# Gate logits of a macaron block from one 16-column product, added by stacked identities

## The reference

```python
x = x + 0.5 * ffn(layernorm(x), ...)
x = x + attn(layernorm(x), ...)
x = x + 0.5 * ffn(layernorm(x), ...)

def ffn(x, gamma1, Wq, bq, Wdown, bdown, Wup, bup, Wo, bo, gamma2, Wg, bg, We):
    h = rmsnorm(x, gamma1)
    q = (h @ Wq + bq).reshape(b, t, 16, 16)
    kv = ((h @ Wdown + bdown) @ Wup + bup).reshape(b, t, 16, 32)
    k, v = split(kv)
    att = softmax(einsum('bthd,btgd->bthg', q, k) / 4)
    out = einsum('bthg,btgd->bthd', att, v).reshape(b, t, 256)
    x = x + (out @ Wo + bo)
    h2 = rmsnorm(x, gamma2)
    gate = softmax(h2 @ Wg + bg)                      # 8 experts, all used
    return x + einsum('btd,edf,bte->btf', h2, We, gate)
```

## Time and profile before

| | |
|---|---|
| timed runs (3) | 1108.99 us median, 1102.47 to 1110.01 |
| the profiled execution | 1103.58 us, span 1101.7 us |
| mean granted TensorE clock | 0.99 of full |
| PE busy | 1031.2 us, 94% |
| DVE busy | 871.4 us, 79% |
| POOL busy | 725.8 us, 66% |
| ACT busy | 653.9 us, 59% |
| DMA moved | 14.30 MB, mean 13 GB/s |

### The profile page before, as it was taken

One profiled execution on the slowest core, in us unless ns is written; L12 is line 12 of the kernel. 1 busy time (PEld: TensorE's weight loads), 2 busy tenths in 40 slices (PEclk: granted clock), 3 DMA queues, 4 the chain that ended last, 5 costly groups with the idle time before them and its releaser, 6 DMA issues. The chain is left out here.

```text
span 1101.7 us, 28470 instructions
## 1 busy us (share of the span) xinstructions
PE 1031.2 (94%) x11320; PEld 779.0 (71%) x11320; DVE 871.4 (79%) x1372; ACT 653.9 (59%) x1331; POOL 725.8 (66%) x727
## 2 busy tenths in 40 slices
PE   4699999999999989999999999877999999999997
PEld 3577878888888855556556556456778788888785
DVE  7888778687785379999998999986886786876853
ACT  4565465565664457767777676654654655655642
POOL 8677476475554348788778887984574664755544
PEclk9899999999999999999999999998999999999999
DMA  6210000000000000000000000000000000000000
GB/s 196 69 40 1 1 2 1 2 1 2 2 2 1 1 1 2 2 1 2 1 1 2 1 2 1 2 1 2 2 2 21 21 2 20 21 1 21 21 1 39
DMA packets 8411, 14.30 MB, mean 13 GB/s; under 512 B 2516, under 2 KB 6102, under 8 KB 8280
## 3 DMA queue, kind: packets, MB, share of 16 engines
q1 hardware_dynamic: 8280, 12.47, 3.4%
HBM read 8.28 MB, written 4.19 MB: 11 GB/s over the span
## 5 line engine op out<-in xcount | busy, mean ns | idle before, releaser
L444 PE MATMUL psum<-we,h 128*128 128x512 f32 x1536 | 397.3, 402 | 0.3 <-DVE X L1062 0.3
L444 PEld LDWEIGHTS psum<-we,h 128*128 128x128 f32 x1536 | 275.6, 188 | 59.4 <-issue 2.3
L1417 POOL TENSOR_TENSOR late<-late 128x512 f32<-128x512 f32 x64 | 82.5, 1290 | 160.0 <-ACT late L1241 160.0
L1241 ACT ACTIVATE late<-psum,gate 128x256 f32<-128x256 f32 x256 | 107.2, 471 | 136.0 <-PE psum L444 96.0
L1089 DVE TENSOR_REDUCE oT<-psum 128x128 fp32r<-128x1024 f32 x128 | 155.5, 1217 | 30.0 <-PE psum L811 30.0
L1062 DVE SCALAR_TENSOR_TENSOR X<-psum,gate,X 128x256 f32<-128x256 f32 x256 | 122.8, 481 | 65.3 <-PE psum L444 55.7
L1291 ACT ACTIVATE kvx<-psum 128x1024 f32<-128x1024 f32 x128 | 131.2, 1025 | 70.5 <-PE psum L821 67.9
L1455 POOL TENSOR_TENSOR kvx<-kvx,late 128x2048 f32<-128x2048 f32 x32 | 124.4, 3887 | 34.3 <-ACT late L1298 34.3
L1095 DVE TENSOR_REDUCE late<-kvx 128x256 f32<-128x2048 f32 x64 | 145.7, 2276 | 0.0
L1455 POOL TENSOR_TENSOR late<-kvx,late 128x2048 f32<-128x2048 f32 x32 | 124.5, 3891 | 29.1 <-ACT late L1298 29.1
L821 PE MATMUL psum<-oT,neg_id 128*128 128x512 f32 x256 | 93.7, 447 | 18.1 <-DVE oT L1089 17.6
(11 more groups left out here) (152 smaller groups left out, 1980.8 us busy)
## 6 DMA issues: line engine op xcount, KB each, us to landing
X<-in_L_attn_hidden_states SPq DMA_DIRECT2D x8, 512.0 KB, 5.9
out<-X SPq DMA_DIRECT2D x8, 512.0 KB, 2.6
X<-in_L_ffn_We SPq DMA_DIRECT2D x2, 1024.0 KB, 10.8
kvx<-in_L_ffn_Wq SPq DMA_DIRECT2D x1, 256.0 KB, 3.2
kvx<-in_L_ffn_Wup SPq DMA_DIRECT2D x2, 128.0 KB, 3.0
kvx<-in_L_ffn_Wo SPq DMA_DIRECT2D x1, 256.0 KB, 4.4
X<-in_L_attn_Wk SPq DMA_DIRECT2D x1, 256.0 KB, 2.8
X<-in_L_attn_Wq SPq DMA_DIRECT2D x1, 256.0 KB, 3.6
```

The source lines that it names most:

```text
L444: ins = e.matmul(out_ap, l, r, start=(n == 0 and not opened), stop=(n == len(terms) - 1), skip_group_check=opened)
L1241: e.activation(y[:, n // 2 * 2 + w, :], psum[:, u % 3, w * D:(w + 1) * D], ACT.Copy, scale=gate[k % 2][:, i, 2 * n + w:2 * n + w + 1]).the ...
L1417: own.step(e.tensor_tensor(y[:, 0:2, :], y[:, 0:2, :], y[:, 2:4, :], ALU.add))
```

## The change

`wg` is laid out so that for each half kk the rounded weights and their rest lie side by side, 16 columns. The gate takes two products for each kk (rounded h2 and the rest of h2, each by all 16 columns) instead of three, into 16 partitions: partitions 0 to 7 hold the part with rounded weights and the bias, 8 to 15 the part with the rest of the weights. (One small term, rest by rest, is now in the sum; before it was left out.) `bgate` has 16 rows, the lower 8 zero. Each transpose of `gateT` becomes an ordinary f32 product of the 16-partition logits with `stack`, two identities of 8x8 above one another, which turns and adds the two parts. `stack` is made by DVE at the start. The DMA of the bias waits for POOL's memset of `bgate`. The planner's numbers become 950 (490 for a half) for `gate` and 330 (220) for `gateT`.

```diff
-            put("PE", size(1400, 720), ("gate", s, w), *(("h2_lo", s, p) for p in own), turned, ("rest_lo", 5))
+            put("PE", size(950, 490), ("gate", s, w), *(("h2_lo", s, p) for p in own), turned, ("rest_lo", 5))
...
-            put("PE", size(300, 200), ("gateT", s, w), ("gate_copy", s, w), last)
+            put("PE", size(330, 220), ("gateT", s, w), ("gate_copy", s, w), last)
...
-        wg = sbt(ctx, "wg", [P, 2, KC, E], F32R)
+        wg = sbt(ctx, "wg", [P, KC, 2, E], F32R)
+        stack = sbt(ctx, "stack", [2 * E, E])
...
-        bgate = sbt(ctx, "bgate", [E, 1])
+        bgate = sbt(ctx, "bgate", [2 * E, 1])
...
-        gT = ct[0:E].rearrange("e g n -> e (g n)")
+        gT = ct[0:2 * E].rearrange("e g n -> e (g n)")
...
-                    terms = [(wg[:, y_, kk, :], h2[k % 2][:, x_, kk, cols]) for kk in range(KC) for x_, y_ in THREE]
-                    product(e, psum[0:E, b, cols], terms).then_inc(s_gl, 1)
+                    terms = [(wg[:, kk, :, :].rearrange("p w e -> p (w e)"), h2[k % 2][:, x_, kk, cols]) for kk in range(KC) for x_ in range(2)]
+                    product(e, psum[0:2 * E, b, cols], terms).then_inc(s_gl, 1)
                 elif name == "gateT":
+                    if k == 0 and piece[2] == 0:
+                        e.wait_ge(s_consts_dve, 5)
                     e.wait_ge(s_gT, done(k, piece[2]))
                     for i in tiles_in(k, piece[2]):
-                        ins = e.transpose(psum[:, b, i * E:(i + 1) * E], gT[:, i * P:(i + 1) * P], ident[0:E, 0:E])
+                        ins = e.matmul(psum[:, b, i * E:(i + 1) * E], gT[:, i * P:(i + 1) * P], stack[:, :], start=True, stop=True,
+                                       skip_group_check=True)
...
             e.tensor_scalar(neg_id[:, :], ident[:, :], -1.0, None, ALU.mult).then_inc(s_consts_dve, 1)
+            e.tensor_tensor(stack[:, :], ident[0:2 * E, 0:E], ident[0:2 * E, E:2 * E], ALU.add).then_inc(s_consts_dve, 1)
...
-                    e.activation(gT[:, cols], psum[0:E, b, cols], ACT.Identity, bias=bgate[:, 0:1]).then_inc(s_gT, 1)
+                    e.activation(gT[:, cols], psum[0:2 * E, b, cols], ACT.Identity, bias=bgate[:, 0:1]).then_inc(s_gT, 1)
...
+            own.step(e.memset(bgate[:, :], 0.0))
...
-            e.dma_start(bgate[:, :], a["L0_ffn_bg"].rearrange("(n o) -> n o", o=1)).then_inc(l_bgate, 16)
+            e.wait_ge(s_const, 2)
+            e.dma_start(bgate[0:E, :], a["L0_ffn_bg"].rearrange("(n o) -> n o", o=1)).then_inc(l_bgate, 16)
```

More of the change, by code:

```diff
@@ L717, in pe_program @@
                     if k == 0 and p == 0:
-                        e.wait_ge(s_consts_dve, 5)
+                        e.wait_ge(s_consts_dve, 6)
                     e.wait_ge(s_ot, 2 * k + p + 1)
@@ L1129, in act_program @@
                 elif piece == ("split_hi", 5):
-                    split_hi(wg[:, 0], raw_g, l_wg, 16)
+                    split_hi(wg[:, :, 0], raw_g, l_wg, 16)
                 elif name == "split_hi" and k >= 8:
@@ L1359, in pool_program @@
                 elif piece == ("rest_lo", 5):
-                    rest_lo(wg[:, 1], raw_g, wg[:, 0], l_wg, 6)
+                    rest_lo(wg[:, :, 1], raw_g, wg[:, :, 0], l_wg, 6)
                 elif name == "rest_lo" and k >= 8:
```

## The result

| | before | after |
|---|---|---|
| timed runs, median (15 each) | 1105.44 us | 1113.75 us |
| lowest to highest | 1102.24 to 1110.23 | 1109.55 to 1120.5 |
| ratio, 95% interval | | 1.0077 [1.0057, 1.0098] |
| span of the profiled execution | 1101.7 us | 1110.8 us |

The change makes the kernel slower by 0.8%, 8.5 us by the ratio. That is inside the stated range and within 1% of no change, but it is clearly not the forecast's +0.6 us. The two profiled executions differ by 9.1 us.

A forecast was written before the change was run, and what follows sets the result against it. PE was taken to bound both feed-forward stages; -7.5 + 10.2 - 1.8 - 0.4 + 0.1 = +0.6 us gave 1104.2 from 1103.58, and the forecast was put at 1107 us, the runs' mean; range 1099 to 1119 (own 1101 to 1113).

The forecast's parts named there:

- The gate: Gate product on PE: 4 products of 512 columns instead of 6, 0.47 us saved a whole job, -7.5 us in all.
- The turning: gateT on PE: 64 transposes become 128 records, loads 0.11 us apart, +0.64 us a whole job, +10.2 us in all.
- rival A: Cheap turning on PE: ordinary 16x128 loads come at 0.061 us, sum -5.7 us, 1100.6 us; chance 0.08.
- B: Serial turning on PE: each load costs its whole 0.188 us, sum +10.6 us, 1117 us; chance 0.06.
- the sum of those terms: Gate product and turning on PE together: -7.5 and +10.2 us.
- the old wait of 0.22: Before, PE loses 0.22 us ahead of expert 3 in each of eight steady jobs, waiting for DVE's add.
- POOL's memset and the DMA behind it: At the start, SP waits for POOL's memset before issuing the gate bias's DMA; claimed to cost nothing.
- the step on the order: Eight steady jobs: the new order shortens the chain to the add, so expert 3's wait goes, -1.8 us.
- a cover of 3.6: PE's work ahead of expert 3: expert 2 (1.5 us), scores (1.03) and attend (1.1), against a chain of 3.2.
- Rival C: DVE's expansions make gate_sub late; expert 3 stalls 1.7 us in eight steady jobs, +16 us, 1122; chance 0.08.
- rival D: The reshuffled line falls into or out of other waits by over 5 us, half each way; chance 0.04.
- the rest of the terms: Outside the steady jobs and jobs 6 and 14: gate and turning, plus late product starts (-0.4 us) and kernel start (+0.1).

The follow-up runs named there:

- e6: The changed kernel with POOL's addition of the bias bo to the base of x1 left out; 1110.17 us, ratio to before 1.004.
- e2: The kernel before, its computation kept, with the planner's numbers 950/490 and 330/220, so in the new order; 1109.42 us, ratio to before 1.0034.
- e18: The changed kernel with four list entries moved in jobs 6 and 14 (PE, ACT and DVE); 1110.81 us, ratio to before 1.0058.
- e1: The changed kernel with only the planner's two old numbers put back, so in the old order; 1107.42 us, ratio to before 1.0033.
- e5: The changed kernel with gateT again by transposes, DVE adding the two halves, and the old planner numbers; 1101.23 us, ratio to before 0.9962.

## Why the prediction was right and where it was wrong

**Right.** PE bounds both feed-forward stages. The gate: 6 products to 4, 0.94 us a job. The turning: two records per product, loads of 186 ns, 0.112 apart in the full line (0.98 us for eight, then `expert 2` starts); rival A (0.061) and B (0.188) are out. With the old order the ratio is 1.0033 [1.0012, 1.0054], which holds the sum of those terms, 2.8 us (1.0025); that a steady job there loses 0.1 us, near the terms' 0.17, owes something to luck, since the old wait of 0.22 had gone in that run too and other products took a little more. POOL's memset and the DMA behind it cost nothing that shows.

**Wrong: the step on the order, "The wait goes: 8 x 0.22 = -1.8 us".** The chain from the turning's end to the `add`'s end was put together from durations that the rows of before give (3.2 us), and set against a cover of 3.6. Its operations had other neighbours after. Measured in seven of the eight steady jobs: 3.8 to 4.0 us, because the scale or the product, 0.17 and 0.19 us, runs beside POOL's bias of 1.28 us and takes up to 1.3. Instead of -0.22 such a job had a wait of 0.4 to 0.6: +0.5 to +0.7 in its step, +4.0 in seven. e6 takes POOL's bias away, the chain falls to 2.9 us and these jobs to about zero, which is the forecast's own -0.05: shown. In the eighth, job 2, the chain took the forecast 3.2 us (scale and product 0.37 and 0.42, beside POOL's `xs` and statistics and not its bias) and the old wait went as foreseen; a wait of 0.52 us for ACT ahead of expert 0 came in its place (+0.7), which no term of the forecast held. What puts ACT late there wasn't tested.

The row of before for L1050 (0.42 us in job 4) was a sign that could have been read: L1034, a subtraction of the same shape ahead of it in the same softmax but with an operand in PSUM, took 0.19. The prediction took no notice of it, and carried the held 0.42 over into its chain of 3.2. The Trainium skill has the rule (SBUF — State Buffer, Who interferes with whom): a DVE instruction with two inputs in SBUF contends with a GpSimd instruction that reads SBUF, DVE's `tensor_scalar` can contend in its two-port modes, and whoever is first holds the shared pair for its whole instruction. The traces here agree in all but the exceptions of the last section, which has the numbers. The kernel's own planner says it too, in its resource `port`.

**Rival C named the right place** (expert 3 late because of the `add`) and the wrong cause: the expansions ahead of `gate_sub`, which it priced at 14 us together. They stand there also in e6, where seven of the eight jobs have no wait left; DVE still waited 0.41 us for the turning at `gate_sub`. The cost was a third of what C gave.

**Not looked at: jobs 6 and 14.** The prediction read one steady job and multiplied by eight. Two jobs at the ends of the stages, where attention's turns come in or no next block follows, had their scores moved behind expert 2 (job 6), or `attend` close behind its exponentials (job 14). They cost 4.7 us. e2 shows this with the old computation, e18 removes 1.4 and 1.1 of it with four entries: shown in that part. What remains (1.1 each) is open. "The rest", rival D, had this at a chance of 0.04; with four in ten of the banks reassigned and 17 rows fewer in PE's list that was far too low.

**The sum.** Forecast +0.6, by the profiles +9.1. The forecast's own terms make a steady job 0.64 - 0.47 - 0.22 = -0.05, eight of them -0.4; measured +4.7, a difference of 5.1. Jobs 6 and 14 were given 0.3 by them and cost 4.7: 4.4. The remaining jobs came out at -0.4 where the rest of the terms makes +0.7: -1.1. Together 8.4, the 8.5 that lie between +0.6 and +9.1.

## What to carry to other kernels

When a change touches a number that a planner reads, run the new computation in the old order and the old computation in the new order before explaining anything; here each gave 0.3%, and the better version (0.9962) was the new product in the old order with transposes kept. A duration read from a trace is that of an instruction beside its neighbours of that trace: before moving it, ask what POOL runs at the new place, and be suspicious of a row that is twice as long as another of the same shape. When an experiment takes a cause out of the new kernel, take it out of the old one too; the difference of the two is what the cause was worth. Look at the jobs at the ends of a stage by themselves, and look at every job for the wait that it has: a steady job times their number leaves out where half of the loss was, and one job that lost as much as its neighbours lost it elsewhere.

## What the runs showed of the hardware that was not expected

**A DVE operation can be held to the end of POOL's instruction.** In after, of the scales (128x4) and products (128x32) of the gate, most take 0.17 and 0.19 us, eight scales 0.37 to 1.28 and three products 0.42 to 1.25. From the traces of before, after and nine experiments I took all scales and products that overlap POOL's bias addition: the 10 products all ended 0.047 to 0.053 us behind it, of 25 scales 23 ended 0.024 to 0.029 behind it, and the other two took their bare 0.17 (one started 0.07 ahead of POOL's instruction, one 0.03 before its end). In before, the product of all eight steady jobs takes 0.415 to 0.418 us and ends 0.04 behind the second of POOL's two L1397 instructions; the scale ahead of it ends 0.02 behind the first. The expansions (128x512) that were held ended 0.28 to 0.30 behind POOL's. A hold can outlast one instruction: in after the expansion at 40.34 took 6.76 us beside eight instructions of POOL's that followed one another without a gap, and ended 0.29 behind the last of them. The reductions (at most 0.19 us), the reciprocal (0.18) and the subtraction, which reads PSUM (0.19), were never held in any of the eighteen traces. The exception: in e1 and e5 eleven scales began 0.07 to 0.13 us behind the start of one of POOL's statistics instructions (L1404 there, L1402 in e5) and took their bare 0.17, while five of e5 that began 0.14 to 0.15 behind were held; I have no explanation for them.

**ACT and DVE rows.** `gate_copy` with 16 partitions took the same 678 ns as with 8. A transpose from 16 partitions into 16 columns loads in 136 ns as one from 8 did.
